# One quarter of the z projection placed ahead of the V transposes at the start of each delta head

## What is computed

```python
qkv = einsum('bth,ch->btc', x, W_qkv)
z   = einsum('bth,vh->btv', x, W_z)
conv = silu(causal_conv4(qkv))              # q, k, v
q, k = l2norm(q), l2norm(k)
def step(state, inp):                       # per head, over the tokens
    state = state * d_t
    delta = (v_t - k_t @ state) * b_t
    state = state + outer(k_t, delta)
    return state, q_t @ state
y = o * silu(z)
y = y * rsqrt(mean(y * y) + 1e-6) * norm_w
out = einsum('btv,ov->bto', y, W_out)
```

## Time and profile before

| | |
|---|---|
| median of 3 runs | 1990.26 us |
| the three runs | 1971.49, 1990.32, 1990.26 us |
| the profiled execution | 1971.39 us, of which its span is 1969.4 us |
| mean granted TensorE clock in it | 0.971 |

### The profile page before, as it was taken

One profiled execution on the slowest core, in us unless ns is written; L12 is line 12 of the kernel. 1 busy time (PEld: TensorE's weight loads), 2 busy tenths in 40 slices (PEclk: granted clock), 3 DMA queues, 4 the chain that ended last, 5 costly groups with the idle time before them and its releaser, 6 DMA issues.

```text
span 1969.4 us, 35372 instructions
## 1 busy us (share of the span) xinstructions
PE 1749.0 (89%) x12824; PEld 1303.0 (66%) x12824; DVE 1519.3 (77%) x2421; ACT 1226.4 (62%) x2155; POOL 636.4 (32%) x442
## 2 busy tenths in 40 slices
PE   7899999999899778889888889888988888988976
PEld 5667676767657566667766667666776666756665
DVE  8788888888674787887777878778777787877853
ACT  3253534444355567777677877768767786777862
POOL 2212222231230535336053261432605326144140
PEclk9999999999999899999999999999999999999988
DMA  3011110101032001101101011010110101101000
GB/s 131 32 62 38 54 61 31 61 31 62 3 99 65 17 16 39 33 23 33 56 23 33 23 34 55 23 34 23 33 55 23 33 23 34 55 23 33 7 1 22
DMA packets 51465, 75.66 MB, mean 38 GB/s; under 512 B 3392, under 2 KB 41792, under 8 KB 51184
## 3 DMA queue, kind: packets, MB, share of 16 engines
q1 hardware_dynamic: 51312, 73.55, 11.7%
HBM read 72.29 MB, written 1.25 MB: 37 GB/s over the span
## 4 chain that ended last, share of the span: by engine, by line
PE 39%; DVE 12%; ACT 10%; issue 9%; POOL 2%; ACTq 0%; DVEq 0%; POOLq 0%
PE bank L897 6%; PE bank L731 6%; PE bank L852 5%; PE bank L742 4%; DVE d_sil L1311 4%; PE bank L790 2%; DVE d_Rb L1377 2%; PE bank L800 2%; PE bank L764 2%; POOL d_dec L1629 2%; DVE d_W L1385 2%; PE bank L873 1%; PE bank L875 1%; PE bank L874 1%; ACT d_TT L1149 1%
## 5 line engine op out<-in xcount | busy, mean ns | idle before, releaser
L1311 DVE SCALAR_TENSOR_TENSOR d_sil<-d_pre,d_w,d_sil 128x1024 f32<-128x1024 f32 x192 | 298.1, 1553 | 5.9 <-ACT d_pre L1081 5.6
L1635 POOL TENSOR_TENSOR d_Rb<-d_V,d_ones 128x512 bf16<-128x512 f32 x32 | 48.0, 1511 | 711.0 <-ACT d_V L1110 711.0
L1363 DVE CAST_PREDICATED d_X<-tables_sb,bank 128x512 bf16<-128x512 int32 x192 | 134.3, 700 | 147.6 <-PE bank L790 146.9
L731 PE MATMUL bank<-xnT,d_w 128*128 128x512 f32 x480 | 244.1, 644 | 0.8
L189 PE MATMUL bank<-xnT,a_w 128*128 128x512 f32 x512 | 237.0, 597 | 0.0
L1145 ACT ACTIVATE d_T<-bank 128x512 bf16<-128x512 f32 x160 | 98.5, 616 | 107.4 <-PE bank L800 105.1
L1629 POOL TENSOR_TENSOR d_dec<-d_dec,d_qk 128x384 f32<-128x384 f32 x128 | 133.2, 1064 | 44.2 <-DVE d_N L1344 44.2
L852 PEld LDWEIGHTS bank<-d_W,d_N 128*128 128x128 f32 x1024 | 122.7, 193 | 35.0 <-DVE d_W L1385 22.4
L189 PEld LDWEIGHTS bank<-xnT,a_w 128*128 128x128 f32 x512 | 90.9, 192 | 78.5 <-issue 78.5
L731 PEld LDWEIGHTS bank<-xnT,d_w 128*128 128x128 f32 x480 | 89.2, 202 | 79.3 <-issue 79.3
L489 POOL TENSOR_TENSOR a_hidc<-a_hid,a_comb 128x512 f32<-128x512 f32 x32 | 44.4, 1387 | 295.0 <-DVE a_hid L336 295.0
(11 more groups left out here) (211 smaller groups left out, 4497.9 us busy)
## 6 DMA issues: line engine op xcount, KB each, us to landing
d_dec<-decay_scratch SPq DMA_DIRECT2D x32, 512.0 KB, 5.7
a_w<-w SPq DMA_DIRECT2D x16, 897.0 KB, 4.6
d_w<-w SPq DMA_DIRECT2D x16, 776.0 KB, 4.8
a_comb<-comb_scratch SPq DMA_DIRECT2D x16, 512.0 KB, 5.5
d_dec<-decay_scratch SPq DMA_DIRECT2D x32, 256.0 KB, 6.0
d_wo<-w SPq DMA_DIRECT2D x16, 256.0 KB, 3.0
f_w<-w SPq DMA_DIRECT2D x8, 256.0 KB, 3.7
tables_sb<-tables SPq DMA_DIRECT2D x1, 1056.0 KB, 8.4
```

The source lines that it names most:

```text
L731: last = pe.matmul(psum[bank][:, :], cols(slot, (c * KT + k) * P, P), xnT[:, k, h * HALF:(h + 1) * HALF], start=(k == 0), stop=(k == KT - 1))
L1311: dve.scalar_tensor_tensor(sil[c][:, :, :], pre[c % 2][:, :, tap:tap + S], cols(slot, OC + 4 * c + tap, 1), sil[c][:, :, :], ALU.mult, ALU ...
L1363: dve.copy_predicated(left(Xp[lv][:, v], lv), mask.unsqueeze(1).broadcast_to([P, 8, 64]).rearrange("p n (g w) -> p n g w", w=lv), psum[4 + ...
```

## The change

The two lines that begin PE's list of a delta head change places. No instruction is added or taken away, the waits of both stay with them, and the lists of DVE, ACT, POOL and SP are the same as before.

```diff
             def body(j, slot, i):
                 nxt = after(j, slot, i)
+                project_z(slot, i, 2)
                 turn_v(i)
-                project_z(slot, i, 2)
                 pe.wait_ge(s["kq_done"], i * 2 + 2)
                 products(i, 0)
                 products(i, 1)
```

## The result

The changed kernel takes 1996.91 us (median of 17 runs, 1990.87 to 2001.13). The kernel before, run as often beside it, takes 1977.56 us (1971.49 to 1991.79). The ratio is 1.008, with a 95% interval of 1.0059 to 1.0102: slower by 0.8%, within the 1% that the prediction called no change. It had given 0.45 to that side of the line and 0.52 to the other, more than 1% slower. The forecast was 1993 us, in a range of 1980 to 2013. The two runs at 1990.3 for which the prediction saw no reason were the upper end of this kernel's spread, whose middle is 1977.6.

The account below looks back on a forecast made before the run. Between products and inversion a head was taken to be set by when DVE begins L1339, not by PE's total. Profiled 1971.4 us + 17.0 (16 heads at 1.06) + 4.9 for the clock gave 1993 us, range 1980 to 2013.

Parts of the forecast that it names:

- PE's order and its own work: Head start on PE: same 20 matrix instructions, own work costs 0; z 1.73 us, then transposes 1.74, products as before.
- ACT: Head start on ACT: first V copy and copy_qk(0) 1.73 us later; the second square moves only 1.06, with DVE's sum.
- DVE: Second gate_z on DVE waits for the later tanh, so L1339 behind it starts 1.06 us later per head.
- POOL: First L1629 on POOL waits for N and moves 1.06 us, 0.12 us behind the end of copy_qk(0).
- rival A: ACT's whole delay carries through, L1629 released by ACT: 1.73 us a head, 2004 us; chance 0.10.
- PE's wait ahead of L790: PE's idle for ACT's copy d_T before L790: 2.32 us, to grow by about 1.06 to some 3.4.
- The clock: L731 groups behind the wait ahead of L790 slow down: three more heads, 4.9 us; at most 9.8 lost, 8.6 back.
- The 1998.2 us: Total by the skill's rule that all six remaining heads get slow groups and nothing returns: 1971.4 + 17.0 + 9.8.
- The sum: Whole kernel: 1971.4 + 17.0 for 16 heads + 4.9 for the clock = 1993 us, 1.1% more; chance 0.65.
- B: Delay hidden, since PE does the same work and idles 2.32 us before L790: 1971 or 1990 us; chance 0.10.
- C: z fills the hole behind the branch, 1.73 us in five heads, 8.7 in all: 1963 us; chance 0.02.
- D: Clock gives back: slow starts behind the branch vanish, 8.6 us, no group gets slow: 1980 us; chance 0.13.

Follow-up runs that it names:

- The dose of the experiments: Kernel before with half a z quarter, one, or two ahead of the V transposes: transposes 0.87, 1.73, 3.46 us later, L1339 0.20, 1.07, 2.80 us later.
- the kernel with half of z: Kernel before with 2 of the z quarter's 4 matmuls ahead of the V transposes, the others behind: 1984.41 us against 1977.36, ratio 1.0022.
- the kernel with z behind the products: Kernel before with z(2) behind both products, ACT's and DVE's lists reordered, both y sums ahead of DVE's last two multiplications: 1999.18 us against 1979.32, ratio 1.0098.
- the kernel with late gates: Changed kernel with DVE's second and third gate_z moved behind its multiplications to N of b = 1: 1985.57 us against 1977.36 before, ratio 1.0028.
- The kernel with twelve more: First kernel with z behind the products, plus 12 added constant transposes per head at PE's wait for d_T: 2018.55 us, ratio 1.02.

## Why the prediction held, step by step

- **PE's order and its own work.** As predicted: z and transposes change places, the products start 1571.59 - 1568.08 = 3.51 us into the head (3.47 before), at 1.73 and about 1.78 us for the two.
- **ACT.** Predicted: idle of 2.88 growing to about 4.6. It was 4.59. The start of `copy_qk(0)` moved by 1.56 (6.67 against 5.11 us into the head) where I had 1.73. Its wait for DVE's sum went from 2.32 to 1.75.
- **DVE.** Predicted: L1339 at 6.04 us and released by its own gate. It was 6.05, and so released. The price, 1.06 a head, held in every head without the branch, and behind it where the start stayed slow (21.07 to 22.20 us up to L790 there, 1.13). The dose of the experiments gives the cover as 0.67 us, which is the 0.58 of idle and the 0.09 by which rows overlap. The sum over the heads, 17.0, is borne out by runs at the same clock, which are 15 to 18 us apart.
- **POOL.** Predicted: L1629 still released by N, and 1.06 later. So it was. `copy_qk(0)` ended at 1575.30, 0.22 us ahead of it, and with DVE relieved it was ACT that released it, so rival A was about as near as the 0.12 us said.
- **PE's wait ahead of L790, the step that failed.** I let it grow to 3.4 us. It stayed at 2.33. What PE does ahead of it is itself released by ACT's copies of the products (L1126), which moved with the chain. The new idle of 0.96 us lies there, ahead of a later L777 group. In the kernel before it was 0.20:

```profile
1557.53 0.67 PE L777 MATMUL bank<-d_sil 128*128 128x256 f32 x2 [0.20 <-ACT d_qk L1126]
```

That group stands 10.55 us into the head after and 9.49 before, the same 1.06 later, and PE works without a gap from it up to the wait. I had followed the chain forward to L790 and not asked what released PE's last work in front of the wait. `products(1)` started 0.20 us later in the head (4.98 against 4.78), as predicted, and it cost nothing.
- **The clock, the term that was mis-sized.** I took three more slow groups, 4.9 us, bounds +9.8 and -8.6. In the profiled execution all six came (8.6 us, at 1.44 and not at my 1.64), the longer low stretches that I had no term for added 5.0, and 3.3 came back behind the branch: +10.3, outside my bounds. In the medians only 19.4 - 17.0 = 2.4 us are left for the clock. The 1998.2 us that I had set beside the rows by the Trainium skill's page came nearer to the measured 1996.91, but by luck: the sum stood on 1971.4, which is 6.2 us below the kernel's median, and its loss of 26.8 us is too large in both measures. The page's example also has longer waits than these. My reason, that a longer idle would bring the slow groups, did not hold: the idle ahead of L790 was as long as before. Even the kernel with half of z, 0.20 us later, had 13 slow groups. What spared every second head in the profiled execution of the kernel before isn't settled.
- **The sum.** Forecast 17.0 + 4.9 = 21.9 on the profiled execution, measured 24.2 there and 19.4 in the medians. The medians hold other clock patterns than the two traces, and the kernel before varies by 20 us from run to run with nothing changed. That 1993 came within 4 us of 1996.91 is in part luck: the base was 6.2 us low and the loss 2.5 us high.
- **The rivals.** A would have shown POOL released by ACT and L1132 1.73 later; it was 1.06. B would have left L1132 where it was. C would have shortened the pause behind the branch by up to 1.73 us a head: the five pauses sum to 9.5 us where they were 11.1, and are issue in both. Over the kernels without added transposes the sum is 9.5 to 10.4 us with z first and 10.8 to 11.3 with V first, so z first shortens it by about 0.2 us a head, an effect that I had at nothing. D happened in part, for 3.3 of its 8.6 us, and was outweighed.

## What to carry to other kernels

When two pieces of work of one engine change places, look at the in-order lists of the engines that consume them: the piece moved back delays all that is queued behind its consumers, up to the cover once and then in full. Before moving work on a second engine to relieve that queue, look at what it releases on a third; here two sums put ahead of DVE's multiplications let its masks fall behind POOL's start, and a gain became a loss. And take the price of a clock from the heads that have it and those that have not, since one pair of executions shows one of its patterns only.

## What was not expected of the hardware

- **DVE's masks beside POOL.** L1356 is a predicated copy from two operands in on-chip memory. Its 32 instructions take 23.3 us before and 69.8 in the kernel with z behind the products; DVE's busy time rose from 1519.3 to 1566.9 us by nearly that alone, with POOL's L1620 or L1621 running beside it. In the kernel with late gates they take 48.7. The groups by line of DVE, z behind the products:

```profile
L1356 DVE CAST_PREDICATED d_TT<-tables_sb,d_N 128x512 bf16<-128x512 int32 x32 | 69.8, 2231 | 0.0
```

The Trainium skill ("SBUF — State Buffer", section "Who interferes with whom") says that a DVE instruction with two inputs in SBUF contends with a GpSimd instruction that reads it, and that the order of issue decides which of them waits. The rows agree with both halves. Where DVE's pair had nearly ended when POOL began (1562.42 and 1563.60 in the kernel before, head 11) it took 1.36 us, and where POOL had begun 0.33 us earlier it took 4.47. In the kernel with late gates DVE's first mask began 0.33 us ahead of POOL and still took 0.74 us, while POOL's instruction beside it took 2.14 instead of 1.89; the second mask, begun behind POOL, took 2.42.
- **The clock falls behind waits of 2.2 to 2.3 us**, in 8 of heads 1 to 14 before and in all 14 after, with the same wait ahead of L790, at 1.44 us for an inversion, or 2.5 where it is low from L790 on. Head 0 was slow in both kernels with no single wait over 1 us there.
- **A second pause behind the loop's branch.** With twenty more PE instructions in each head, PE pauses again 1 to 2 us into the head, for 1.6 to 3.3 us in the changed order and 2.2 to 3.2 in the old one (L1339 8.9 to 11.8 us behind the first instruction there). The kernel with twelve more has it too, for 0.3 to 2.2 us. The traces point at PE's code and not at its data. In the nine kernels without added transposes two 16 KB transfers of the instruction queue have landed 1.5 us or more before the head's first PE instruction, in each of the five heads. In the three with them only one has; the next lands 1.8 to 4.0 us into the head, and in 15 heads of 15 PE goes on 1.3 to 1.6 us behind it. SP's transfers of the decay run at that time and may delay it. No kernel with the code moved was run, so this is read from the traces and not shown by experiment.
